# Order of one block's gate and up against the last half of a scan unit on VectorE, where a two-layer mixture-of-experts kernel passes from layer one to layer two

## The chip, the cores and the metric

The kernel runs on one NeuronCore of a Trainium2 chip. The metric is the device time of one execution in microseconds (us), lower is better, given as the median of several runs. Engines are named as in the profile: PE is TensorE (PEld its weight loads), DVE is VectorE, ACT is ScalarE, POOL is GpSimd, SP is SyncE, which issues most DMAs. Each engine has its own queue of instructions, and engines wait for each other through semaphores.

## The reference

Two layers, each of a condition (a scan over time in both directions) and a feed-forward part with routed experts. x has 4 x 512 tokens of 512 features, fside 4 x 512 rows of 512 features.

```
x = x + L0_ffn(L0_cond(x, fside, fside, w, u, cond), ...)
x = x + L1_ffn(L1_cond(x, fside, fside, w, u, cond), ...)

cond(r, k, v, w, u, time_emb):
    decay = exp(-exp(w)) * (0.5 + 0.5 * tf)          # tf = sigmoid(sum(time_emb))
    ek = exp(min(k, 30)); ekv = ek * v               # here k = v = fside
    nf, df = forward scans  a = a * decay + ekv,  b = b * decay + ek
    nb, db = the same scans backwards
    euk = exp(min(u + k, 30))
    num = nf + nb - ekv + euk * v
    den = df + db - ek + euk
    return sigmoid(r) * (num / max(den, 1e-8)) * (0.8 + 0.2 * tf)

L0_ffn: h = rmsnorm(x) * weight; top 2 of 8 experts of inner size 256, plus a shared expert
L1_ffn: top 6 of 32 experts of inner size 352 (at most 512 tokens each), plus a shared one of 704
expert(t): (silu(t @ w_gate) * (t @ w_up)) @ w_down
```

The scans depend on fside alone, not on x, so those of layer two can be computed while the experts of layer one still run.

## The kernel before, in words

**Blocks.** All feed-forward work is cut into 215 blocks n of 128 rows and one expert each. n = 0 to 15 are the shared blocks of the first layer, n = 16 to 54 its 39 routed blocks (j = n - 16, `R0` = 16, `S1` = 55), n = 55 to 86 the shared ones of the second layer, n = 87 to 214 its 128 routed ones. In the code the first layer is l = 0, so the last routed block of layer one is n = 54 = `S1 - 1`, j = 38.

**A block's stages** are spread over the engines. `gu_pe`: TensorE multiplies the turned rows with the gate and up weights (L1831) into the PSUM bank psG. Values are held as a high and a low float16 half, so there are three matmuls where one would stand. `gu`: ScalarE takes the tanh of the gate half (L1243), and VectorE makes H with two products (L1650 and L1652). `h_turn`: TensorE transposes H (L1844), and ScalarE rounds it to the high half HS (L1253). `h_low`: TensorE subtracts it (L1857), and ScalarE writes the low half (L1261). `down`: TensorE multiplies HS with the down weights (L1880) into psO, ScalarE writes OB (L1278), and SyncE stores OB to the DRAM array of slots (L984).

**Units.** The scans are cut into 32 units u of 128 features by 512 times, 16 to each layer. A unit's first half is `k_fwd` and `k_bwd`, four scans on VectorE (L1341, L1345, L1352, L1355) with scalings between them on ScalarE. Its second half, `second_half(u)`, is `k_den` on VectorE (L1362 and L1365, whose semaphore is k_euv), `k_num` on GpSimd (L1013), `k_rec`, the reciprocal on VectorE (L1370), and `k_out` on VectorE (L1377). Between them stand k_min, k_mul and k_load of later units, of which there are none for u = 31, the last. `k_turn` transposes the unit's result on TensorE (L1696) and ScalarE copies it to RT (L1142), which raises the semaphore k_rt.

**The order** is written out by hand. The generator `stages()` (from L119) yields one list of stages, and each engine walks through that list and issues the stages that it has a part in. So an engine's queue follows this list, and moving a stage moves it for every engine that has a part in it, and for no other. In the loop over the routed blocks of layer one (from L405), iteration j yields among others gu_pe of block n, then `turn_made()` (k_turn of a unit finished in an earlier iteration), `next_half()` in those iterations in which a half is due, h_turn of block n - 1, gu of block n, `after_half()`, h_low of n - 2 and down of n - 3. `next_half()` takes the halves in turn through the counter `half`, yields one of them, and after a second half notes the unit in `made` for the following `turn_made()`. 27 halves are due in the 39 iterations; the last of them, in j = 38, is the second half of unit 31. For the iterations from 39 on, in which only h_turn, h_low and down are still to be done, no half is left. So at the end the list reads:

```
gu_pe 54 | k_den 31, k_num 31, k_rec 31, k_out 31 | h_turn 53 | gu 54 | h_low 52 | down 51 | w_load 34
k_turn 31 | h_turn 54 | h_low 53 | down 52
h_low 54 | down 53
down 54
y_load 0 to 3 | pick 0, 1 | w_hi 27, w_lo 27, ... w_hi 34, w_lo 34 | x_sum 0 | f_tanh 16 | gate 16 ...
```

**What comes behind.** ScalarE's `w_hi` 27 (L1224) begins to split the weights of layer two into halves, and waits for down 54, whose weights it writes over; VectorE's `w_lo` (L1631) makes the low half of each. `pick` (L1085) has GpSimd gather the two routed results of each token, and waits for the last stores to the slots and for k_rt 32 (k_turn 31). `y_load` waits for k_rt too. `x_sum` (L1397) adds them up on VectorE, and the tanh, the gate and the transposes of layer two's first tile follow.

Of the kernel before, what the change touches and what calls it, by code (L numbers as in the profile page):

```python
# [34 lines left out]
R0, S1, R1, NBLK = 16, 55, 87, 215  # L35
# [83 lines left out]
def stages():  # L119
# [3 lines left out]
    def loads(n, upto):  # L123

        for _ in range(n):
            k = RING[done["load"]] if done["load"] < len(RING) else len(PIECES)
            if k < upto and done["load"] < sum(j < done["lo"] for j in RING) + 2:
                yield "w_load", k
                done["load"] += 1
# [30 lines left out]
    def second_half(u, piece=()):  # L160
        yield "k_den", u
        if u + 1 < 32:
            yield "k_min", u + 1
        yield "k_num", u
        if u + 1 < 32:
            yield "k_mul", u + 1
        yield from piece
        if u + 2 < 32:
            yield "k_load", u + 2
        yield "k_rec", u  # L170
# [4 lines left out]
    def turn_made():  # L175
        while made:
            u = made.pop()
            yield "k_turn", u
            if u in (19, 23):
                yield "k_store", u // 4  # L180

    def next_half():
        u, second = divmod(half[0], 2)
        if u >= 32:
            return
        half[0] += 1
        if second:
            yield from second_half(u)
            yield "k_out", u
            made.append(u)  # L190
        else:
            yield "k_fwd", u
            yield "k_bwd", u

    def after_half():

        u, second = divmod(half[0], 2)
        if second and raised[0] < u + 1 < 32:
            raised[0] = u + 1
            yield "k_exp", u + 1  # L200
# [204 lines left out]
    for j in range(NB0 + 3):  # L405
        n = R0 + j
        if n + 3 < S1:
            yield "gather", n + 3
        if n + 2 < S1:
            yield "x_turn", n + 2  # L410
        if n < S1:
            yield "gu_pe", n
        yield from turn_made()
        if j * 27 // 39 != (j - 1) * 27 // 39 or j >= 39:
            yield from next_half()
        if n - 1 < S1:
            yield "h_turn", n - 1
        if n < S1:
            yield "gu", n
        yield from after_half()  # L420
        if n - 2 < S1:
            yield "h_low", n - 2
        if 1 <= j:
            yield "down", n - 3
        if j in (20, 22, 24, 26):
            yield "w_load", 27 + (j - 20) // 2
        if j == 28:
            yield from loads(2, 43)
        if j in (36, 38):
            yield "w_load", 33 + (j - 36) // 2  # L430
# [133 lines left out]
    for j in range(NB1 + 2):  # L564
        n = R1 + j
# [28 lines left out]
def build(nc, xtok, fT, cst, svec, cond, rout, gatew, W0, W1, Y1):  # L594
    with ExitStack() as ctx:
# [285 lines left out]
        def _(eng):  # L881
# [112 lines left out]
            for what, n in stages():  # L994
                if what in mine:
                    mine[what](n)

        @block.gpsimd
        def _(eng):
# [91 lines left out]
            for what, n in stages():  # L1091
                if what in mine:
                    mine[what](n)

        @block.scalar
        def _(eng):
# [186 lines left out]
            for what, n in stages():  # L1283
                if what in mine:
                    mine[what](n)
# [662 lines left out]
```

## Time and profile before

| | |
|---|---|
| median of 3 runs | 1552.21 us |
| lowest and highest | 1548.61 and 1553.45 us |
| the profiled execution, its own time | 1552.92 us |
| its span, first to last instruction | 1551.1 us |
| mean granted TensorE clock | 0.955 of full speed |
| PE busy | 1327.5 us (86%) |
| DVE busy | 1001.7 us (65%) |
| ACT busy | 729.6 us (47%) |
| POOL busy | 582.7 us (38%) |
| chain that ended last, by engine | PE 69%, DVE 21%, issue 5%, ACT 2%, DMA 2% |

The chain is the work that ended last, followed back from the last instruction to whatever released each piece. "issue" in it is time in which an engine waited for nothing that the profile shows. Busy time is an average over very different stages: up to 500 us the scans and layer one's blocks run beside each other, around 500 to 525 us the kernel passes from layer one to layer two, and from there on it is mostly matmuls. In the timeline, times are from the start of the span.

### The profile page before, as it was taken

The numbers are of one execution on the slowest core, as the hardware profiler recorded it, in microseconds if no ns is written. First come the engines' busy times: TensorE is split into PE (matmuls) and PEld (weight loads), VectorE is DVE, ScalarE is ACT, GpSimd is POOL, SyncE is SP. The second block draws the span as 40 slices with busy tenths as digits, with TensorE's granted clock in tenths as the row PEclk, the third lists the DMA queues.
The fourth block names the chain that finished last, engine by engine and source line by source line (L and its number), as shares of the span: only waits on it lengthen the run. The fifth ranks groups of instructions, "written<-read, shape, count | busy, mean of one in ns | idle before, by whom it ended". The sixth has DMA issues, their size and how long they took to land.

```text
span 1551.1 us, 23666 instructions
## 1 busy us (share of the span) xinstructions
PE 1327.5 (86%) x8228; PEld 807.3 (52%) x8228; DVE 1001.7 (65%) x1760; ACT 729.6 (47%) x1251; POOL 582.7 (38%) x454
## 2 busy tenths in 40 slices
PE   0047565699999599999899999999999999999997
PEld 0023252244444366666566666666666666666664
DVE  8999988978888568878644444444444444444432
ACT  3466663645545443221254445445444454454432
POOL 2343443443442344110144444444444444444443
PEclk9987966899999799999999999999999999999999
DMA  3556546678896585441368999889899899989974
GB/s 104 171 163 202 145 116 135 131 184 184 217 245 174 166 214 167 112 116 50 110 163 198 203 202 209 197 205 207 200 209 199 203 209 197 207 202 199 211 142 75
DMA packets 224178, 269.12 MB, mean 174 GB/s; under 512 B 148608, under 2 KB 148736, under 8 KB 223936
## 3 DMA queue, kind: packets, MB, share of 16 engines
q1 hardware_dynamic: 187408, 175.58, 43.6%
q0 software_dynamic: 36656, 92.03, 29.2%
q8 instruction: 70, 1.15, 0.3%
q14 instruction: 44, 0.36, 0.1%
HBM read 167.87 MB, written 70.32 MB: 154 GB/s over the span
## 4 chain that ended last, share of the span: by engine, by line
PE 69%; DVE 21%; issue 5%; ACT 2%; DMA 2%; POOL 0%; SPq 0%; POOLq 0%; DVEq 0%; ACTq 0%
PE psG L1831 39%; PE psO L1880 21%; DVE wkFD L1370 5%; PE psH L1848 3%; DVE wkFD L1352 2%; PE psX L1792 2%; DVE wkFN L1345 2%; DVE wkFD L1341 2%; DVE wkFN L1377 1%; DVE wkFN L1355 1%; DVE wkFD L1362 1%; DVE H L1650 1%; PE psX L1730 1%; DVE Wlo L1631 1%; PE psX L1719 1%
## 5 line engine op out<-in xcount | busy, mean ns | idle before, releaser
L1831 PE MATMUL psG<-Whi,XSp 128*128 128x352 f16 (+2 forms) x3000 | 668.3, 328 | 11.5 <-issue 9.6
L1831 PEld LDWEIGHTS psG<-Whi,XSp 128*128 128x128 f16 x3000 | 294.7, 99 | 209.8 <-issue 36.4
L1880 PE MATMUL psO<-Whi,HS 128*128 128x512 f16 (+1 forms) x1180 | 390.5, 383 | 0.5 <-DVE OB L1670 0.5
L1831 PE MATMUL psG<-Wlo,XSp 128*128 128x352 f16 (+2 forms) x1500 | 387.4, 328 | 0.0
L1071 POOL DMA_INDIRECT out<-OB,posb x128 | 202.8, 1585 | 410.3 <-ACT OB L1278 410.3
L1631 DVE SCALAR_TENSOR_TENSOR Wlo<-ST,Whi 128x1088 f16<-128x1088 f32 (+1 forms) x124 | 160.0, 1291 | 229.9 <-ACT Whi L1224 229.9
L1650 DVE SCALAR_TENSOR_TENSOR H<-H,psG 128x352 f32<-128x352 f32 (+1 forms) x215 | 105.5, 491 | 210.5 <-ACT H L1243 210.5
L1880 PE MATMUL psO<-Wlo,HS 128*128 128x512 f16 (+1 forms) x590 | 226.2, 383 | 0.0
L1243 ACT ACTIVATE H<-psG 128x352 f32<-128x352 f32 (+1 forms) x215 | 95.3, 443 | 230.3 <-PE psG L1831 230.3
L1831 PEld LDWEIGHTS psG<-Wlo,XSp 128*128 128x128 f16 x1500 | 148.8, 99 | 92.7 <-issue 7.1
L1880 PEld LDWEIGHTS psO<-Whi,HS 128*128 128x128 f16 x1180 | 117.1, 99 | 118.1 <-issue 5.2
L1053 POOL DMA_INDIRECT XG<-xrows,posb x128 | 129.2, 1009 | 122.1 <-DVE posb L1562 74.2
L1278 ACT ACTIVATE OB<-psO,WSL 128x512 f32<-128x512 f32 x128 | 88.0, 688 | 183.8 <-PE psO L1880 183.8
L1224 ACT ACTIVATE Whi<-ST 128x1088 f16<-128x1088 f32 (+1 forms) x124 | 136.1, 1098 | 0.0
L1652 DVE SCALAR_TENSOR_TENSOR H<-H,psG 128x352 f32<-128x352 f32 (+1 forms) x215 | 106.4, 495 | 7.4
L1660 DVE TENSOR_TENSOR HS<-psH,HS 128x384 f16<-128x384 f32 x160 | 88.1, 550 | 33.2 <-ACT HS L1256 33.1
L1013 POOL TENSOR_TENSOR wkFN<-wkFN,wkEU 128x512 f32<-128x512 f32 x32 | 40.6, 1268 | 181.1 <-DVE wkEK L1332 169.9
L1256 ACT CAST HS<-psH 128x384 f16<-128x384 f32 x160 | 75.6, 473 | 69.5 <-PE psH L1848 69.5
L1370 DVE RECIPROCAL wkFD<-wkFD 128x512 f32<-128x512 f32 x32 | 107.0, 3345 | 0.0
L1696 PE MATMUL psX<-C,wkFN 128*128 128x128 f32 x64 | 16.4, 405 | 102.1 <-DVE wkFN L1377 102.1
L1880 PEld LDWEIGHTS psO<-Wlo,HS 128*128 128x128 f16 x590 | 58.2, 99 | 47.8 <-issue 1.7
L1848 PE MATMUL psH<-C,H 128*128 128x128 f32 x480 | 78.6, 273 | 1.1 <-DVE H L1652 1.1
(219 smaller groups left out, 1505.7 us busy)
## 6 DMA issues: line engine op xcount, KB each, us to landing
ST<-W SPq DMA_DIRECT2D x130, 544.0 KB, 5.1
ST<-W SPq DMA_DIRECT2D x23, 512.0 KB, 4.0
slots<-OB SPq DMA_DIRECT2D x39, 256.0 KB, 3.2
wkK<-fT SPq DMA_DIRECT2D x32, 256.0 KB, 3.7
xrows<-XG SPq DMA_DIRECT2D x20, 256.0 KB, 2.9
y0rows<-x SPq DMA_DIRECT2D x8, 512.0 KB, 5.4
y0rows<-OB POOLq DMA_DIRECT2D x16, 256.0 KB, 5.1
out<-OB SPq DMA_DIRECT2D x16, 256.0 KB, 2.4
```

The lines of the kernel that those rows point to most:

```text
L1053: G.indirect_dma_start(out=XG[g % 3][:, 0:w], out_offset=None, in_=X[l][:, :], in_offset=bass.IndirectOffsetOnAxis(ap=idx[l][:, j:j + 1], ...
L1071: G.indirect_dma_start(out=Y1[:, :], out_offset=bass.IndirectOffsetOnAxis(ap=idx[1][:, j:j + 1], axis=0), in_=OB[o % 4][:, :], in_offset=N ...
L1224: op = A.activation(st if who == "pool" else hi, st, ACT.Copy, scale=WS)
L1243: A.activation(H32[a][:, 0:F], psG[a][0][:, 0:F], ACT.Tanh, scale=0.5 * UN).then_inc(b_tanh, 1)
L1370: V.reciprocal(FD[n % 2][:, :], FD[n % 2][:, :]).then_inc(k_rec, 1)
L1631: op = V.scalar_tensor_tensor(out=Wlo[:, at:at + cw], in0=st, scalar=WS, in1=Whi[:, at:at + cw], op0=ALU.mult, op1=ALU.subtract)
L1650: V.scalar_tensor_tensor(out=H, in0=H, scalar=1.0, in1=g, op0=ALU.add, op1=ALU.mult).then_inc(b_sil, 1)
L1652: V.scalar_tensor_tensor(out=H, in0=H, scalar=(-0.5, 0.5)[l] * XS * UN * UN, in1=u, op0=ALU.mult, op1=ALU.mult).then_inc(b_h, 1)
L1660: V.tensor_tensor(hs(n)[:, 1, 0:w], psH[:, 0:w], hs(n)[:, 0, 0:w], ALU.subtract).then_inc(b_hslo, 1)
L1831: op = M.matmul(o, hx[:, x, q * P:q * P + P], w(half_, off + c, nn), start=first, stop=last)
L1848: op = M.transpose(bank_[:, q * P:q * P + P], H32[a][:, q * P:q * P + P], ident)
L1880: op = M.matmul(psO[bank(o)][:, :], hs(n)[:, x, q * P:q * P + P], columns[n](half_, off0 + q * 512, 512), start=(q == 0 and x == 0 and hal ...
```

## The change

Where a half is due in the iteration of block 54 (j = 38), `next_half()` is yielded after `gu` of the block and not ahead of `h_turn` of the block before. All other iterations keep their order.

```diff
         yield from turn_made()
-        if j * 27 // 39 != (j - 1) * 27 // 39 or j >= 39:
+        due = j * 27 // 39 != (j - 1) * 27 // 39 or j >= 39
+        if due and n != S1 - 1:
             yield from next_half()
         if n - 1 < S1:
             yield "h_turn", n - 1
         if n < S1:
             yield "gu", n
+        if due and n == S1 - 1:
+            yield from next_half()
         yield from after_half()
```

The list then reads, in the iteration of block 54: gu_pe 54, h_turn 53, gu 54, k_den 31, k_num 31, k_rec 31, k_out 31, h_low 52, down 51, w_load 34. The lines below it are as before.

## Rows read from the trace of the kernel before

**Rows 1.** Chain of waits, 494 to 532 us: start us, us, engine, tile, line.

```profile
496.99 0.70 DVE wkFD L1362
...
503.31 0.44 PE psH L1844 x2
...
510.06 1.11 ACT Whi L1224
...
511.19 8.08 DVE Wlo L1631 x7
...
521.01 0.67 DVE wkK L1397
```

**Rows 2.** Timeline of VectorE: start us, us, engine, line, operation [idle before <- releaser].

```profile
490.84 0.42 DVE L1650 SCALAR_TENSOR_TENSOR H<-H,psG 128x256 f32<-128x256 f32 x1 [1.23 <-ACT H L1243]
...
491.63 1.22 DVE L1341 TENSOR_TENSOR_SCAN wkFD<-dec,wkEK 128x512 f32<-128x512 f32 x1
...
496.66 0.42 DVE L1652 SCALAR_TENSOR_TENSOR H<-H,psG 128x256 f32<-128x256 f32 x1
...
501.77 0.69 DVE L1377 SCALAR_TENSOR_TENSOR wkFN<-wkFD,wkFN 128x512 f32<-128x512 f32 x1
...
502.83 0.42 DVE L1652 SCALAR_TENSOR_TENSOR H<-H,psG 128x256 f32<-128x256 f32 x1
```

**Rows 3.** Timeline of ScalarE: tanh of blocks 52 and 54, h_low 52, OB 54.

```profile
490.42 0.39 ACT L1243 ACTIVATE H<-psG 128x256 f32<-128x256 f32 x1
...
498.84 0.38 ACT L1243 ACTIVATE H<-psG 128x256 f32<-128x256 f32 x1
499.11 0.39 ACT L1261 ACTIVATE HS<-psH 128x256 f16<-128x256 f32 x1
...
509.57 0.60 ACT L1278 ACTIVATE OB<-psO 128x512 f32<-128x512 f32 x1 [0.70 <-PE psO L1880]
```

**Rows 4.** Timeline of TensorE: end of down 51, k_turn 31, h_turn 54, end of down 54.

```profile
499.55 0.38 PE L1880 MATMUL psO<-Whi,HS 128*128 x1
502.52 0.66 PE L1696 MATMUL psG<-C,wkFN 128*128 128x128 f32 x4 [2.59 <-DVE wkFN L1377]
503.31 0.44 PE L1844 MATMUL psH<-C,H 128*128 128x128 f32 x2
...
509.15 0.38 PE L1880 MATMUL psO<-Whi,HS 128*128 x1
```

**Rows 5.** Timeline of TensorE: k_turn of unit 29 and the h_turn behind it.

```profile
474.96 0.60 PE L1696 MATMUL psG<-C,wkFN 128*128 128x128 f32 x4
475.39 0.38 PE L1844 MATMUL psH<-C,H 128*128 128x128 f32 x2
```

**Rows 6.** Windows: stretch, us, PE, PEld, DVE, ACT, POOL busy, granted clock, DMA share, GB/s.

```profile
275.00:276.00 1.00, 0.00 (x0) 0.00 (x0) 0.58 (x1) 1.00 (x3) 0.74 (x1) 0.69 0.00 0
282.00:283.00 1.00, 1.00 (x6) 0.57 (x5) 1.00 (x1) 0.22 (x2) 1.00 (x1) 0.89 0.94 258
309.00:310.00 1.00, 0.00 (x0) 0.00 (x0) 0.96 (x3) 0.00 (x0) 0.71 (x1) 0.76 0.84 49
316.00:317.00 1.00, 1.00 (x7) 0.61 (x6) 0.00 (x0) 0.27 (x1) 0.00 (x0) 0.83 0.64 231
504.00:505.00 1.00, 1.00 (x4) 0.30 (x3) 0.00 (x0) 0.45 (x2) 0.00 (x0) 0.54 0.12 48
507.00:508.00 1.00, 1.00 (x5) 0.42 (x4) 0.00 (x0) 0.00 (x0) 0.00 (x0) 0.75 0.43 170
```

**Rows 7.** Timeline of TensorE: two wakings behind longer idle time.

```profile
277.71 0.40 PE L1857 MATMUL psH<-HS,ident 128*128 128x256 f16 x1 [5.22 <-ACT HS L1253]
...
311.17 0.60 PE L1831 MATMUL psG<-Whi,XSp 128*128 x1 [6.72 <-issue]
```

**Rows 8.** Timeline of GpSimd: k_num of unit 31 and the first pick.

```profile
498.55 1.27 POOL L1013 TENSOR_TENSOR wkFN<-wkFN,wkEU 128x512 f32<-128x512 f32 x1 [11.12 <-DVE wkEU L1365]
...
512.96 1.57 POOL L1085 DMA_INDIRECT wkFD<-slots,sl  x1 [13.14 <-DMA slots<-OB]
```

## The prediction

> **What bounds the kernel now.** The page of the profile gives the first direction: TensorE carries 69% of the chain that ended last and VectorE 21%, so an edit on VectorE counts only where VectorE stands on that chain. The second view is the chain of waits around the last routed block of the first layer, block 54 [rows 1]. There VectorE is on the path: k_den of unit 31 at 496.99, then its reciprocal and k_out, then TensorE's turn of H for block 54 at 503.31, the down matmuls, the first split of the next layer's weights on ScalarE at 510.06, seven and then one more low half on VectorE from 511.19, and x_sum at 521.01. The reader is to see that nothing on this stretch is a wait for a DMA or a fixed time: each piece starts 0.02 to 0.45 us behind the one before it. The third view is the timeline of each engine over the same stretch, which says what stands in each queue.
>
> VectorE [rows 2]: the second product of gu 53 ends at 496.66 + 0.42 = 497.08, k_den of unit 31 starts at 496.99 [rows 1] (records overlap by about 0.1 us), k_out starts at 501.77 and ends at 502.46, and gu 54 ends at 502.83 + 0.42 = 503.25. No instruction of these waits. ScalarE [rows 3]: the tanh of gu 54 starts at 498.84 and ends at 499.23. TensorE [rows 4]: down 51 ends at 499.93, then TensorE idles for 2.59 us until k_turn 31 at 502.52, released by k_out; h_turn 54 follows at 503.31, right behind gu 54 on the chain [rows 1]; down 52, 53 and 54 end at 509.15 + 0.38 = 509.53.
>
> The point that decides is the order on TensorE. The stage list puts k_turn 31 (through `turn_made` of j = 39) in front of h_turn 54, h_low 53 and down 52. The diff moves no item of TensorE. So TensorE waits first for k_out 31 and only then for gu 54, and the change makes the second of these two early at the cost of the first.
>
> **The change part by part.** Only VectorE gets another order. The half that moves has k_den, k_rec and k_out for VectorE and k_num for GpSimd; for u = 31 it has no k_load, k_mul, k_min or k_exp. On GpSimd, ScalarE, SyncE and TensorE the moved half passes only items they don't carry (h_turn and gu are not on GpSimd or SyncE, and the half is not on the other two), so their orders stay, w_load and the store of j = 38 among them.
>
> *The wait that is added.* gu 53 needs no more than before and ends at 497.08. Behind it now stands gu 54, which waits for the tanh. Nothing of VectorE's later work feeds that tanh, so it stays where it is and ends at 499.23. From the end of such a tanh to VectorE's start it is 490.84 - (490.42 + 0.39) = 0.03 us [rows 2, 3]; I take 499.26, rounded to 499.25. VectorE thus idles from 497.08 to 499.25, 2.17 us, with k_den, k_euv, k_rec and k_out of unit 31 queued behind the waiting instruction. GpSimd's k_num 31 waits for k_euv (today it starts at 498.55 [rows 8]), and TensorE's k_turn 31 waits for k_out.
>
> *The two products in front.* The pair of a block on an idle VectorE takes 491.63 - 490.84 = 0.79 us up to the start of the next instruction [rows 2]. So k_den starts at 500.04 in place of 496.99, +3.05 us.
>
> *The second half itself.* From k_den's start to k_out's end it takes 502.46 - 496.99 = 5.47 us [rows 1, 2], k_num included, since 1.27 us of GpSimd from just behind k_euv lies beside the reciprocal. k_out ends at 505.51, and k_turn 31 starts 0.06 us behind it as now, at 505.57: +3.05.
>
> *What is given back.* h_turn 54 finds its H long ready. Two units earlier k_turn and h_turn stand without a wait, 475.39 - 474.96 = 0.43 us apart [rows 5], where here they are 503.31 - 502.52 = 0.79 us apart [rows 4]. So 0.36 us comes back, and h_turn 54 starts at 506.00: +3.05 - 0.36 = +2.69 us. All that follows hangs on it: down 54, ScalarE's OB at 509.57 and the split behind it [rows 3], the low halves, and GpSimd's first pick, which waits for the stores of OB until 512.96 [rows 8]. I cost all of that at zero change of duration and a shift of 2.69.
>
> *The cover for the tail.* Work that TensorE does between 499.93 and 505.57 would hide the delay. down 52 is such work: the low half of its H leaves ScalarE at 499.11 + 0.39 = 499.50 [rows 3]. It stands behind k_turn 31, and in the trace of before TensorE already idles for 2.59 us with it in the queue [rows 4]. The Trainium skill, "TensorE: Matmul & The Clock Gate", Step-by-step: what each phase is for, says that only weight loads are pulled ahead and matmuls stay in program order. By that rule the early H stays unused and the sum below stands; without it the sum would be that of the second rival, about -3 us. The trace agrees as far as the 2.59 us of idle go.
>
> *The clock.* TensorE's idle time grows from 2.59 to 5.64 us. The granted clock now falls at 504.08 (0.54 in the stretch 504 to 505) and is back at 507.50 (0.75 in 507 to 508) [rows 6]: 3.42 us at 0.5, which is 1.2 in place of 2.4 GHz, and so 1.71 us lost in down 52 and 53. The nearest longer idle stretches: behind 5.22 us of idle TensorE woke at 277.71 [rows 7], with the clock low from 275.38 to 282.22 [rows 6], 4.51 us of it after waking; behind 6.72 us it woke at 311.17 [rows 7], low until 316.34 [rows 6], 5.17 us. I take the first, nearest in idle time: 4.51 / 2 = 2.26 us lost, +0.55 us on now. Bounds: if the clock comes back at 507.50 as now, (507.50 - 505.57) / 2 = 0.97 is lost, -0.74 us. If the whole stretch runs low: it has 509.53 - 502.52 - 0.36 - 1.71 = 4.94 us of work at full clock, so 4.94 is lost, +3.23 us.
>
> *Sum.* +3.05 - 0.36 + 0.55 = +3.24 us, between +1.95 and +5.92. The profiled execution took 1552.92 us (span 1551.1 and 1.8 around it), so it would take 1556.16. It stands 0.71 above the median of the runs, 1552.21; against the median the forecast is 1555.5.
>
> **The rivals.** *The clock makes it more than 0.3% slower.* The 0.3%, 4.66 us, is about what a measurement of this kernel can tell from no change. This needs a clock term of 4.66 - 2.69 = 1.97 us or more, that is (1.97 + 1.71) x 2 = 7.4 us at 1.2 GHz after 505.57. The longest such stretch above is 5.17 us, which speaks against it; but TensorE idles again between down 54 and the next layer's first tile, which the chain reaches only behind x_sum at 521.01 [rows 1], and if it wakes there to a longer low stretch than now, a second loss of up to 1.7 us (what one low stretch costs now) would do it. Time with the whole stretch low: 1552.21 + 5.92 = 1558.1. Chance 0.17.
>
> *TensorE profits from the early H.* If h_turn 54 and the downs ran before k_turn 31, they would start at 500.1, just behind gu 54, without the 2.59 us idle and without its clock loss; k_turn 31 at 505.57 and ScalarE's copy of it would become last, some 1.3 us long, so the split starts near 507 and not at 510.06: about -3 us, 1549.1. The stage list and the idle time in [rows 4] speak against it. Chance 0.02.
>
> *The second half is not held back.* If VectorE took k_den 31 while gu 54 waits for its tanh, k_out would end near 502.46 as now, or 0.79 us later: 0 to +0.4 us, at most 1552.7. No row of before shows VectorE with ready work behind a wait of this kind at this place. The Trainium skill, same page, "Architectural detail", calls VectorE strict first in, first out; by that rule the sum above stands. Chance 0.01.
>
> *The delay is taken up later.* If something behind 510 waits for what isn't shifted, part or all of the 3 us goes: 1552.2 to 1553.5. For it: VectorE idles 7.94 us before its first low half (503.25 to 511.19), and TensorE long before the next layer. Against it: both idle stretches end by work on this very chain [rows 1], and the picks and stores hang on down 54 too [rows 8]. Chance 0.10.
>
> **How the numbers follow.** The forecast, slower by 2 to 4.6 us, has 0.70. Within 0.3% lie it, the delay taken up later and the unheld half, 0.81 together; slower by more is 0.17; faster by more than 0.3% would take the case in which TensorE profits and a lucky spread, 0.02. The range reaches down below full absorption, since the three runs alone go from 1548.61 to 1553.45, to 1551.3; up it takes in the whole stretch at low clock (1558.1) and some of a second cold start, to 1559.3.
>
> **What would show it.** In the profile of the changed kernel VectorE should idle about 2.2 us in front of gu 54; k_den 31 should start some 3 us later against gu 53's end; TensorE should idle about 5.6 us before k_turn 31, and h_turn 54 should follow it by 0.43 us at full clock (twice that at half). The first split on ScalarE should start 2 to 6 us later than 510.06, and the rest of the timeline be shifted by the same. The prediction is wrong if h_turn 54 stands ahead of k_turn 31 in TensorE's order, if VectorE does not idle before gu 54, or if the shift at the first x_sum differs from that at the end by more than 2 us.

## The result and the profile after

The changed kernel takes 1555.99 us (median of 21 runs, 1553.66 to 1559.33); the kernel before takes 1552.21 (median of 21 runs, 1548.61 to 1556.51). The ratio is 1.0029 with a 95% interval of 1.0021 to 1.0037, so the change costs 4.5 us, between 3.3 and 5.7. Its profiled execution took 1554.51 us with a span of 1552.7. Two slow runs, 2323.33 us in e2 and 7805.0 us in e4, are left out of the ratios of the experiments below.

A difference of two spans says little here: the profiled execution of the changed kernel came to block 53 some 2.5 us earlier than that of before (its first product on VectorE starts at 493.72 against 496.23), where the two kernels are the same; the kernel before itself reaches it at 496.23, 496.06 and 494.16 in three profiles. So all shifts below are counted from that start, called gu 53. VectorE's timeline answers [rows 2]; start us, us, engine, line, operation, idle before and its releaser. The engines' lines have numbers 3 higher than before.

```profile
494.15 0.42 DVE L1655 SCALAR_TENSOR_TENSOR H<-H,psG 128x256 f32<-128x256 f32 x1
496.75 0.42 DVE L1653 SCALAR_TENSOR_TENSOR H<-H,psG 128x256 f32<-128x256 f32 x1 [2.18 <-ACT H L1246]
497.20 0.42 DVE L1655 SCALAR_TENSOR_TENSOR H<-H,psG 128x256 f32<-128x256 f32 x1
497.54 0.68 DVE L1365 SCALAR_TENSOR_TENSOR wkFD<-wkEU,wkFD 128x512 f32<-128x512 f32 x1
...
502.32 0.69 DVE L1380 SCALAR_TENSOR_TENSOR wkFN<-wkFD,wkFN 128x512 f32<-128x512 f32 x1
512.64 1.29 DVE L1634 SCALAR_TENSOR_TENSOR Wlo<-Whi 128x1088 f16<-128x1088 f32 x1 [9.63 <-ACT Whi L1227]
```

VectorE now idles 2.18 us for the tanh of gu 54, then does the two products, and only at 497.54 begins k_den of unit 31. k_out ends at 503.01, 9.29 us behind gu 53; before it was 502.46 - 496.23 = 6.23. TensorE, answering [rows 4]:

```profile
497.04 0.38 PE L1883 MATMUL psO<-Whi,HS 128*128 x1
503.06 1.11 PE L1699 MATMUL psG<-C,wkFN 128*128 128x128 f32 x4 [5.64 <-DVE wkFN L1380]
503.97 0.63 PE L1847 MATMUL psH<-C,H 128*128 128x128 f32 x2
...
510.60 0.38 PE L1883 MATMUL psO<-Whi,HS 128*128 x1
```

The first line is the end of down 51. TensorE then idles 5.64 us where it idled 2.59. h_turn 54, whose H has been ready since 497.62, starts at 503.97, behind k_turn 31. The windows of this stretch answer [rows 6]; the third number from the right is the granted clock:

```profile
502.00:503.00 1.00, 0.00 (x0) 0.00 (x0) 0.90 (x2) 0.00 (x0) 0.00 (x0) 0.62 0.00 0
...
509.00:510.00 1.00, 1.00 (x6) 0.44 (x5) 0.00 (x0) 0.28 (x1) 0.00 (x0) 0.96 0.55 215
```

A mean of 0.62 over 502 to 503 leaves 0.76 us of it at half speed, and 0.96 over 509 to 510 leaves 0.08; between them every stretch of 1 us has 0.50. So the clock is at 1.2 GHz from 502.24 to 509.08, 6.02 us of it behind k_turn's start at 503.06. The chain of waits, answering [rows 1], shows that all the rest follows as before:

```profile
503.06 1.11 PE psG L1699 x4
504.18 0.43 PE psH L1847 x2
...
507.59 3.40 PE psO L1883 x12
...
511.51 1.11 ACT Whi L1227
...
512.64 8.04 DVE Wlo L1634 x7
...
522.45 0.68 DVE wkK L1400
```

k_turn 31 now stands on the chain where [rows 1] went from gu 54 to h_turn 54. The times behind gu 53, all from the timelines of the profiles (`b` the kernel before, `a` the changed one, each with two further profiles from the experiments):

```
                     b      b_look b_look2  a      a_look a_look2
k_out 31 ends        6.23   6.23   6.24     9.29   9.29   9.29
k_turn 31 starts     6.29   6.29   6.29     9.34   9.35   9.35
h_turn 54 starts     7.08   7.07   7.08     10.25  10.26  10.26
last down ends       13.30  13.30  11.62    17.26  15.67  16.16
first split (ACT)    13.83  13.83  12.15    17.79  16.20  16.69
first x_sum          24.70  24.70  23.02    28.65  27.07  27.56
first turn, layer 2  29.06  29.06  27.38    33.01  31.43  31.92
from there to end    1025.8 1026.0 1026.0   1026.0 1028.9 1025.6
```

### The profile page after: what moved, and what is told of

Its sections match the earlier page's. It is cut to its first block, busy times and chain, and to the rows that moved or that the text cites. A ratio compares the mean times of both kernels' runs of the same rounds, so it can differ in the third digit from the quotient of the medians.

```text
span 1552.7 us, 23666 instructions
## 1 busy us (share of the span) xinstructions
PE 1327.8 (86%) x8228; PEld 806.3 (52%) x8228; DVE 1001.3 (64%) x1760; ACT 729.4 (47%) x1251; POOL 580.7 (37%) x454
## 4 chain that ended last, share of the span: by engine, by line
PE 72%; DVE 21%; issue 5%; ACT 2%; POOL 0%; DMA 0%; POOLq 0%; SPq 0%; DVEq 0%; ACTq 0%
PE psG L1834 41%; PE psO L1883 22%; DVE wkFD L1373 5%; PE psH L1851 3%; DVE wkFD L1355 2%; PE psX L1795 2%; DVE wkFN L1348 2%; DVE wkFD L1344 1%; DVE wkFN L1380 1%; DVE wkFD L1365 1%; DVE wkFN L1358 1%; PE psX L1733 1%; DVE Wlo L1634 1%; DVE H L1653 1%; PE psX L1722 1%
```

## The experiments

**How much of the delay is the wait, and how much the products.** In e1 gu 54 stands between the reciprocal and k_out, where its tanh is long done; in e2 between k_euv and the reciprocal.

The two edits of the changed kernel, drawn as one (each run has one of the two marked lines):

```diff
-        if n < S1:
+        if due and n == S1 - 1:
+            yield "k_den", 31
+            yield "k_num", 31
+            yield "gu", n        # only in e2
+            yield "k_rec", 31
+            yield "gu", n        # only in e1
+            yield "k_out", 31
+            half[0] += 1
+            made.append(31)
+        elif n < S1:
             yield "gu", n
-        if due and n == S1 - 1:
-            yield from next_half()
```

> gu 54 stands between the reciprocal and k_out of unit 31, where its tanh is long done, so the added idle time is gone and only the two products (0.79 us) stand in front of k_out. Theory (idle 2.17 + products 0.79, then TensorE's order): counted from gu 53 on VectorE, k_turn 31 starts 0.8 us later than before, h_turn 54 0.4 us later, TensorE's last down the same give or take the clock; total +0.4 us, between -0.5 and +1.5. Rival (the loss has nothing to do with how late k_out is, but with gu 54 standing ahead of it): about +3.8 us as in the changed kernel. Rival (an early H is worth something by itself): below -1 us.

> gu 54 stands between k_euv and the reciprocal of unit 31; VectorE waits for the tanh from about 498.4 to 499.25 in the times of the kernel before. Theory: k_out later by 0.9 idle + 0.8 products = 1.7 us, h_turn 54 later by 1.3 us, and TensorE idles 4.3 us before k_turn 31; with the clock term total +1.3 to +2.8 us, between the kernel before and the changed one. Rival (loss not in proportion to k_out's delay): +3.8 us, or none.

e1 measured 1.0002 (0.9986 to 1.0018), which is +0.3 us (-2.2 to +2.8); e2 1.0019 (1.0005 to 1.0032), +2.9 us (+0.8 to +5.0), just above the expected +2.8. VectorE in e1, then in e2:

```profile
499.29 0.36 DVE L1659 SCALAR_TENSOR_TENSOR H<-H,psG 128x256 f32<-128x256 f32 x1
499.68 0.42 DVE L1661 SCALAR_TENSOR_TENSOR H<-H,psG 128x256 f32<-128x256 f32 x1
500.02 0.68 DVE L1386 SCALAR_TENSOR_TENSOR wkFN<-wkFD,wkFN 128x512 f32<-128x512 f32 x1
```

```profile
496.08 0.42 DVE L1659 SCALAR_TENSOR_TENSOR H<-H,psG 128x256 f32<-128x256 f32 x1 [0.85 <-ACT H L1252]
496.54 0.42 DVE L1661 SCALAR_TENSOR_TENSOR H<-H,psG 128x256 f32<-128x256 f32 x1
496.88 3.34 DVE L1379 RECIPROCAL wkFD<-wkFD 128x512 f32<-128x512 f32 x1
```

With no wait the products cost k_out 0.54 us (6.77 behind gu 53). The expected 0.8 was too much: the pair takes 500.02 - 499.29 = 0.73 us, and it starts 3.27 us behind the reciprocal's start, where k_out started 3.45 behind it before. With a wait of 0.85 us k_out ends at 7.95, +1.72 as expected. With the wait of 2.18 us in the changed kernel it is +3.06. So the delay of k_out follows the wait, with 0.87 and 0.88 us on top of it, and h_turn 54 follows k_out: it starts at 7.33, 8.92 and 10.25 or 10.26. gu 54 ahead of k_out does little harm by itself: e1's interval ends below the +3.8 us of the rival that put the loss on its place. The other rival, a gain of over 1 us from an early H, is not dropped by e1's interval, but h_turn 54 starts 0.25 us later than before there, so its early H was not used.

**The clock.** e3 is the changed kernel and e4 the kernel before, each with spare matmuls in TensorE's idle time; what they write isn't used.

```diff
             def k_turn(n):
                 bank_ = k_bank(n)
+                if n == 31:
+                    for _ in range(24):      # e3; 11 in e4
+                        M.matmul(psG[1][1][:, 0:512], ident16[:, :], XSp[xslot(S1 - 1) % 4][:, 0, :],
+                                 start=True, stop=True)
                 eng.wait_ge(k_out, n + 1)
```

> The changed kernel with 24 spare matmuls of 512 columns (about 5.2 us at full clock) between down 51 and k_turn 31 on TensorE; their result is not used. Theory (2.69 us of delay plus a clock loss of 3.0 where before loses 1.7): the clock stays at 1.0 after 502, k_turn 31 starts no later than in the changed kernel, and TensorE's last down ends 1.0 us later than in the kernel before, counted from gu 53: total +1.0 us, -2.8 against the changed kernel. Rival (the clock is not part of it): still +3.5 to +4.

> The kernel before with 11 spare matmuls of 512 columns (2.4 us) between down 51 and k_turn 31; their result is not used. Theory: the clock stays at 1.0 through down 52 and 53, the last down ends 1.7 us earlier; total -1.7 us. Rival (the drop of the clock comes from elsewhere, or its loss is hidden): 0.

e3 measured 1.0006 (0.9992 to 1.0021), +0.9 us against before, where the changed kernel without the spare matmuls has 1.0029. Its interval ends at +3.3 us, just below the rival's +3.5, so the profile is the firmer sign. e4 measured 0.9990 (0.9976 to 1.0004), -1.6 us, an interval that just holds zero and with it the rival; there too the profile decides. In e3 TensorE's timeline and two windows read:

```profile
499.01 5.34 PE L1693 MATMUL psG<-XSp,ident 128*128 128x512 f16 x24
504.81 0.66 PE L1703 MATMUL psG<-C,wkFN 128*128 128x128 f32 x4 [0.46 <-DVE wkFN L1380]
505.31 0.38 PE L1851 MATMUL psH<-C,H 128*128 128x128 f32 x2
```

```profile
499.00:504.00 5.00, 5.00 (x25) 2.25 (x23) 4.93 (x4) 0.60 (x1) 1.27 (x1) 1.00 0.49 164
504.00:510.00 6.00, 5.33 (x28) 2.56 (x26) 0.69 (x1) 2.88 (x7) 0.00 (x0) 1.00 0.13 48
```

The delay of k_out is whole (9.28 behind gu 53), the granted clock stays at 1.00, and the last down ends at 14.32. In e4 it ends at 11.63. The difference, 2.69 us, is the pure delay, with the clock at 2.4 GHz on both sides. What the changed kernel has above 14.32 is its clock loss: 2.94, 1.35 and 1.84 us in its three profiles. e2 and e1 lie between. In e1 the clock stays up, and the last down ends at 11.81. In e2 it ends at 15.20, with the clock low up to 505.62, 4.55 us behind the start of k_turn 31 at 501.07:

```profile
505.00:506.00 1.00, 1.00 (x5) 0.45 (x4) 0.00 (x0) 0.58 (x2) 0.00 (x0) 0.69 0.00 0
```

Half of that, 2.3 us, is lost, so an estimate without the loss is 12.9. The last down then ends at 11.6, 11.8, 12.9 and 14.3 us behind gu 53 for delays of k_out of 0, 0.54, 1.72 and 3.06 us.

**How firm the clock term is.** Each kernel was profiled twice more, as it is.

> The kernel before once more, for a second profile of it. What is open is the size of the clock term: one profile of each kernel has shown 3.4 us at 1.2 GHz before (1.7 us lost) and 6.0 us after (3.0 lost). If 3.4 us is what this idle time of 2.6 us always brings, it shows again, with the last down 13.3 us behind gu 53. If it depends on the run, this profile may show none of it, and the last down 11.6 us behind gu 53.

> The changed kernel once more. A fixed clock loss gives the last down 17.3 us behind gu 53 again. If it depends on the run, anything from 14.3 (none) to 17.3 us; with a low stretch that ends 4.5 us after waking, as the prediction took it, 16.5.

> The kernel before, a third profile: the last down 13.3 us behind gu 53 if the clock always falls there, 11.6 if it doesn't in this run.

> The changed kernel, a third profile: the clock falls in any case after 5.6 us of idle time; the last down between 15.2 and 17.3 us behind gu 53.

Their executions took 1552.87 and 1549.31 us (before) and 1557.32 and 1554.49 us (changed). The windows of b_look2:

```profile
500.00:504.00 4.00, 3.42 (x19) 1.96 (x20) 1.15 (x3) 2.10 (x5) 0.00 (x0) 1.00 0.45 144
504.00:508.00 4.00, 1.78 (x9) 0.59 (x6) 0.55 (x1) 2.78 (x4) 0.00 (x0) 1.00 0.51 198
```

Behind the same 2.59 us of idle time the clock did not fall before the last down had ended, which it does at 11.62 and not at 13.30. The changed kernel's low stretch in a_look and in a_look2:

```profile
503.00:504.00 1.00, 0.00 (x0) 0.00 (x0) 0.90 (x2) 0.00 (x0) 0.00 (x0) 0.95 0.06 22
507.00:508.00 1.00, 1.00 (x6) 0.39 (x5) 0.00 (x0) 0.00 (x0) 0.00 (x0) 0.85 0.00 0
```

```profile
501.00:502.00 1.00, 0.00 (x0) 0.00 (x0) 1.00 (x1) 0.00 (x0) 0.81 (x1) 0.74 0.89 147
508.00:509.00 1.00, 1.00 (x5) 0.45 (x4) 0.00 (x0) 0.33 (x1) 0.00 (x0) 0.85 0.00 0
```

It ends 2.8 and 3.8 us behind k_turn 31 (504.52 in both), and half of that is lost, 1.4 and 1.9 us. So the clock loss differs between executions of one kernel: 1.7, 1.7 and 0 before, 2.9, 1.4 and 1.8 after, by mean 1.1 and 2.0.

**Where the early H went.** v1 and v2 move k_turn 31 behind down 54, v1 in the changed kernel and v2 in the kernel before.

```diff
-        yield from turn_made()
+        if n < S1:
+            yield from turn_made()
```

> The changed kernel with k_turn 31 (TensorE and ScalarE) behind down 54 in place of ahead of h_turn 54. Theory (the early H was lost in TensorE's queue): h_turn 54 starts right behind gu 54, some 3 us earlier than in the kernel before counted from gu 53, TensorE doesn't idle over 1.5 us, the clock stays up, the last down ends 4.5 to 5 us earlier than before; k_turn 31 is 3.05 us later and ScalarE's copy of it ends last, so the first split of the weights starts about 3 us earlier than before: total -3 us, -7 against the changed kernel. Rival (k_out's own delay reaches the end by another way, such as the picks that wait for it): +3 us.

> The kernel before (gu 54 behind the second half on VectorE) with k_turn 31 behind down 54. Theory: h_turn 54 starts at the same point as before, released by gu 54, TensorE idles 3.3 us in front of it; k_turn 31 and its copy of 1.3 us now lie behind the last down: total +0.9 us, between 0 and +2.5 with the clock. Rival (k_turn's place is what matters, not the early H): as v1, about -3 us.

v1 measured 0.9986 (0.9973 to 1.0000), -2.2 us; v2 1.0005 (0.9993 to 1.0018), +0.8 us. TensorE and ScalarE in v1:

```profile
499.57 0.44 PE L1848 MATMUL psH<-C,H 128*128 128x128 f32 x2 [0.26 <-DVE H L1656]
...
503.73 0.38 PE L1884 MATMUL psO<-Whi,HS 128*128 x1
504.96 0.66 PE L1700 MATMUL psG<-C,wkFN 128*128 128x128 f32 x4 [0.85 <-DVE wkFN L1381]
```

```profile
504.15 0.60 ACT L1282 ACTIVATE OB<-psO 128x512 f32<-128x512 f32 x1 [0.70 <-PE psO L1884]
505.65 0.69 ACT L1146 ACTIVATE RT<-psG,cs 128x512 f32<-128x512 f32 x1 [0.91 <-PE psG L1700]
506.24 1.10 ACT L1228 ACTIVATE Whi<-Whi 128x1088 f16<-128x1088 f32 x1
```

k_out ends as late as in the changed kernel (9.29 behind gu 53), but h_turn 54 starts at 3.96 in place of 10.26, TensorE hardly idles, and the last down ends at 8.50. The copy of k_turn 31 is last, and the first split starts at 10.63, 3.2 us earlier than in the first profile of before and 2.6 earlier than the mean of its three (13.27); the rest of the 3.2 is that profile's clock loss. v2 shows that the place of k_turn alone isn't it: its h_turn 54 stays at 7.08, behind an idle time of 3.38 us that gu 54 ends.

```profile
501.31 0.44 PE L1845 MATMUL psH<-C,H 128*128 128x128 f32 x2 [3.38 <-DVE H L1653]
```

So the same edit of VectorE's order costs 4.5 us with k_turn 31 ahead of h_turn 54, and turns v2's +0.8 into v1's -2.2, a gain of 3 us, with k_turn 31 behind it. The two intervals against the kernel before overlap, but set against each other the 12 times of v1 and the 12 of v2 differ in their means by 3.0 us, with a 95% interval of about 1 to 5.

v3 is v1 with the first split of the weights also ahead of k_turn 31.

```diff
+    yield from splits(1)
     yield from turn_made()
...
-    yield from splits(8)
+    yield from splits(7)
```

> As v1_turn_last, with the first split of the next layer's weights (w_hi and w_lo 27) also ahead of k_turn 31. Theory: ScalarE starts this split as soon as the last down ends, 5 us earlier than before, its copy of k_turn 31 follows within 1.1 us, and VectorE's eight low halves end 4.5 us earlier than before: total -4.5 us, -1.4 against v1. Rival (the picks, which wait for k_turn 31 and the stores, then end last): as v1, -3 us.

It measured 0.9977 (0.9965 to 0.9990), -3.6 us, and is faster than both kernels, if by 0.23% only. The interval, -5.4 to -1.6 us, holds the expected -4.5 and the rival's -3. ScalarE:

```profile
504.50 1.10 ACT L1229 ACTIVATE Whi<-Whi 128x1088 f16<-128x1088 f32 x1
505.51 0.69 ACT L1147 ACTIVATE RT<-psG,cs 128x512 f32<-128x512 f32 x1
506.10 1.10 ACT L1229 ACTIVATE Whi<-Wlo 128x1088 f16<-128x1088 f32 x1
```

The split starts 9.02 behind gu 53, and x_sum at 20.28, 4.4 us earlier than in the first profile of before and 3.9 earlier than the mean of its three. Against v1 the split starts 1.6 us earlier and x_sum 1.2; the timings of the two, 1.4 us apart, do not resolve that. The picks did not become last: x_sum starts right behind the last low half, with no idle time of VectorE between them, which drops the rival.

**Filling the idle time of the kernel before.** v4 lets TensorE do h_low 53 and down 52 ahead of k_turn 31, with VectorE's order as before.

```diff
+        if n == S1:
+            yield "h_low", n - 2
+            yield "down", n - 3
         yield from turn_made()
...
-        if n - 2 < S1:
+        if n - 2 < S1 and n != S1:
             yield "h_low", n - 2
-        if 1 <= j:
+        if 1 <= j and n != S1:
             yield "down", n - 3
```

> The kernel before with h_low 53 and down 52 ahead of k_turn 31 in the list, VectorE's order as before. Theory: 1.4 us of work fills part of the 2.6 us that TensorE idles; what is behind h_turn 54 gets 1.4 us shorter and the clock may not fall (another 1.7 us): total -1.4 to -3.1 us, with h_turn 54 at its old place. Rival (TensorE's idle time is not on the path): 0.

It measured 1.0003 (0.9992 to 1.0015), so no gain over 1.2 us. That misses the expectation. Its profile has TensorE and the clock as follows:

```profile
501.18 0.66 PE L1699 MATMUL psG<-C,wkFN 128*128 128x128 f32 x4 [1.19 <-DVE wkFN L1380]
501.96 0.44 PE L1847 MATMUL psH<-C,H 128*128 128x128 f32 x2
502.88 0.28 PE L1860 MATMUL psH<-HS,ident 128*128 128x256 f16 x1 [0.48 <-ACT HS L1256]
```

```profile
499.00:506.00 7.00, 5.04 (x24) 2.13 (x22) 2.77 (x4) 3.15 (x8) 0.00 (x0) 1.00 0.50 155
```

The last down ends at 10.96, only 0.66 us earlier than the 11.62 of before without a clock loss: what down 52 freed behind h_turn 54 is in part a wait of 0.48 us for ScalarE's copy of H 54. Against the mean of before's three profiles, (13.30 + 13.30 + 11.62) / 3 = 12.74, this would be -1.8 us; the timing doesn't show that much. e4 measured -1.6 us although its last down ends 0.67 us later than v4's, so the spread of 12 runs is as large as what is asked here. The difference stays open.

**What the rest of the span adds.** The last row of the table is 1025.6 to 1026.0 in five profiles and 1028.9 in a_look, and of the experiments e4 and v1 have 1028.3 and 1028.9 (the other experiments 1025.5 to 1026.9). These three are of three different kernels, and one of them, e4, has VectorE's order of before. The 3 us come in at two places, which ScalarE's tanh of each block shows.

The first is where TensorE wakes for layer two. In every profile the clock is low there, and how long it stays low differs: 5.1 to 6.2 us behind the first turn in the other five profiles of the table, 8.0 in a_look, 7.7 in e4 and 7.9 in v1. The first tanh of layer two starts 7.9 to 8.5 us behind the first turn in those five and at 9.36, 9.21 and 9.30 in these three. The stretch in which the clock comes back, in a_look (first turn at 526.60) and in b_look (525.12):

```profile
534.00:535.00 1.00, 1.00 (x6) 0.57 (x5) 0.00 (x0) 0.00 (x0) 0.00 (x0) 0.69 0.93 349
```

```profile
530.00:531.00 1.00, 1.00 (x7) 0.53 (x5) 0.42 (x1) 0.00 (x0) 0.00 (x0) 0.68 0.98 344
```

The second is where layer two's shared blocks give way to its routed ones. There the clock fell in these three profiles and in none of the other eleven, and from the tanh of block 83 to that of block 87, the first routed one, it takes about 17.0 us in each of them, in place of 15.4 or 15.5 in the other profiles of the table. The windows of v1, and of the kernel before at the same place:

```profile
751.00:752.00 1.00, 0.63 (x5) 0.56 (x6) 0.32 (x2) 0.00 (x0) 0.00 (x0) 0.61 0.00 0
754.00:755.00 1.00, 1.00 (x5) 0.39 (x4) 0.00 (x0) 0.00 (x0) 0.85 (x1) 0.69 0.54 70
```

```profile
754.00:755.00 1.00, 0.93 (x8) 0.58 (x9) 0.47 (x3) 0.00 (x0) 0.00 (x0) 1.00 0.00 0
```

The clock is low for 3.4 us there, which at half speed is 1.7 us, near the 1.6 that it takes longer. The two places together are 2.8 us in a_look against b_look, of 2.9. That the low clock makes them wasn't tried by an experiment of its own. They are a reason not to set a single profile's span against another's here, v1's 1550.4 against 1551.1 for instance.

## Why the prediction was right, step by step

- **VectorE's order and nothing else:** TensorE's order around k_turn 31 and h_turn 54 is as before in the profile of after, as the prediction said.
- **The added wait:** 2.17 us was worked out, 2.18 measured. k_out and k_turn 31: +3.05 worked out, +3.06 and +3.05 measured.
- **What is given back:** +2.69 us was worked out as the shift with the clock left out. e3 less e4 gives 14.32 - 11.63 = 2.69. That the last digit fits is luck: at full clock h_turn 54 follows k_turn 31 by 0.50 us (e1, e3) and not by the 0.43 of [rows 5], so h_turn 54 is delayed by 9.84 - 7.08 = 2.76, and another 0.07 comes back behind it.
- **The clock:** this term was mis-sized. It was +0.55, from one low stretch of 4.51 us after waking and one loss of 1.71 us in the profile of before. In the profile of after 6.02 us were low, outside the 4.51 to 5.17 us of the neighbours in [rows 6, 7], though inside the outer bound; its term is (17.26 - 14.32) - 1.68 = +1.26. By the means over three profiles each it is +0.9 (2.0 less 1.1). By these means the loss after was near the 2.26 that was taken for it, and the step that failed is to take the 1.71 us before as certain: the clock falls there in two profiles of three.
- **The cover and the tail:** first split, first x_sum and first turn of layer two are shifted by 3.96, 3.95 and 3.95 us between the first profiles of the two kernels. The whole shift is kept to the end, and nothing took it up. That drops the rival of a delay that is taken up later. Counted in the times of the two spans the first split starts only 511.51 - 510.06 = 1.45 us later, below the 2 to 6 us named as a sign; the sign holds only when counted from gu 53. In a_look the shift against the first profile of before grows from 2.4 us at the first x_sum to 5.5 at the end, past the 2 us that the prediction allowed; what it gains there came in e4 too, with VectorE's order of before.
- **The sum:** +3.24 us was forecast. The timings say 4.5 (3.3 to 5.7), the medians differ by 3.8, and the shift at the last down, by the means, is 16.36 - 12.74 = 3.6. 2.7 of it is the delay, 0.9 the clock. Up to the end of the span the means of three profiles are 4.5 us apart: 0.4 more comes in where TensorE wakes for layer two, most of it from a_look alone, and 0.5 where the shared blocks end, all of it from a_look. Whether the change has a part in this last 0.9 us isn't shown. The forecast was low by 0.4 to 1.3 us, and that 1555.5 stands only 0.5 below the measured median owes something to chance.
- **The rivals:** VectorE did not pass its wait. TensorE did not take h_turn 54 ahead of k_turn 31, and v1 shows what it would have been worth if it had: the split 3.2 us earlier than in the first profile of before, where the prediction had 3, and -2.2 us by the timings. The clock made the change cost more than expected. The ratio, 1.0029, stands just under the 0.3% of the first rival and its interval reaches over it to 1.0037, so the timings do not drop that rival. The traces show its second loss, behind x_sum, in one profile of three: a_look's first tanh of layer two is 1.2 us later behind the first turn than b_look's.

## What to carry to other kernels

An early result is worth something only if its consumer's queue can reach it: before moving a producer forward, read what stands ahead of the consumer on its own engine, and move that too. Where two results are needed one behind the other, delaying the first to bring the second forward costs the whole wait that the second carries, here 2.18 of the 3.06 us by which k_out was late. A gap of idle time on TensorE has a price of its own in clock, and it differs from one execution to the next, so price such a term from several profiles.

## What was not expected of the hardware

The same idle time does not always lower the granted clock: behind 2.59 us of idle TensorE it fell in two profiles and stayed in one, behind 3.38 us (v2) and 4.31 us (e2) it fell, and in e1 it stayed at 1.00 behind 3.12 us:

```profile
500.76 0.66 PE L1705 MATMUL psG<-C,wkFN 128*128 128x128 f32 x4 [3.12 <-DVE wkFN L1386]
```

```profile
498.00:506.00 8.00, 4.98 (x26) 2.57 (x26) 2.67 (x4) 3.19 (x8) 0.00 (x0) 1.00 0.41 138
```

Behind 5.6 us it fell in all three profiles, and was low for 2.8 to 6.0 us after waking. Where layer two's shared blocks give way to the routed ones, TensorE is idle for the same 2.21 us in all 14 profiles; the clock fell there in three of them, for 3.4 us each, and stayed at 1.00 in eleven.
